# The skip term D*xi of a state-space block: added to y by VectorE instead of being scaled on ScalarE and transposed into the sum on TensorE

## The reference

```python
xi = silu(conv.transpose(0, 2, 1))
...
h = da * h + dbu                    # the scan over time, for 16 states
y = ys.transpose(1, 0, 2) + xi * Dp # the skip term
y = y * silu(z)
return jnp.einsum('bse,de->bsd', y, op_w)
```

## Time and profile before

| what | before |
|---|---|
| median of three runs (lowest, highest) | 8749.79 us (8738.89, 8761.13) |
| span of the profiled execution | 8758.3 us |
| VectorE busy | 6915.6 us, 79% |
| TensorE matmul busy, weight load busy | 7541.7 us (86%), 5200.9 us (59%) |
| GpSimd busy | 6082.7 us, 69% |
| ScalarE busy | 5521.0 us, 63% |
| mean granted TensorE clock | 0.943 of full |

### The profile page before, as it was taken

How to read it: one execution, slowest core, us unless ns; L and a number is a source line. 1 busy time by engine, 2 the same in 40 slices (tenths; PEclk the granted TensorE clock), 3 DMA queues, 4 the chain that set the end, 5 groups by cost and what they waited for, 6 DMA issues and landing times. The chain is left out here.

```text
span 8758.3 us, 163471 instructions
## 1 busy us (share of the span) xinstructions
PE 7541.7 (86%) x67488; PEld 5200.9 (59%) x67488; DVE 6915.6 (79%) x6906; ACT 5521.0 (63%) x8491; POOL 6082.7 (69%) x3204
## 2 busy tenths in 40 slices
PE   7886788888888888888888888888889888888879
PEld 4664466666664666666654666666654666666655
DVE  5887788888875588888875688888874688888873
ACT  5665676666654566666653666666654666667643
POOL 5883488888871588888861588888861588888861
PEclk8997899999999999999999999999999999999989
DMA  1111111111100111111100111111100111111100
GB/s 62 51 51 63 41 46 43 46 43 51 56 28 25 55 46 43 46 48 56 48 32 20 53 46 43 46 52 56 43 32 22 52 46 43 53 55 46 43 32 15
DMA packets 133156, 388.71 MB, mean 44 GB/s; under 512 B 49580, under 2 KB 78188, under 8 KB 95552
## 3 DMA queue, kind: packets, MB, share of 16 engines
q1 hardware_dynamic: 132416, 378.25, 12.0%
HBM read 364.97 MB, written 13.24 MB: 43 GB/s over the span
## 5 line engine op out<-in xcount | busy, mean ns | idle before, releaser
L1167 DVE TENSOR_TENSOR_SCAN arena<-arena,ps 128x512 f32<-128x512 f32 x4608 | 5493.0, 1254 | 1019.2 <-issue 822.1
L1418 POOL TENSOR_TENSOR arena<-arena 128x1024 f32<-128x1024 f32 x2240 | 5262.7, 2363 | 1115.4 <-DVE arena L1167 1087.0
L863 ACT ACTIVATE arena<-arena,rate 128x512 f32<-128x512 f32 (+1 forms) x4608 | 3040.6, 713 | 583.8 <-DVE arena L1167 579.3
L572 PEld LDWEIGHTS ps<-csts,arena 128*128 128x128 f32 x17920 | 2115.6, 146 | 514.3 <-issue 423.0
L572 PE MATMUL ps<-csts,arena 128*128 128x128 f32 x17920 | 2354.8, 283 | 4.8 <-POOL arena L1418 4.7
L555 PE MATMUL ps<-arena 32*128 32x128 f32 x36864 | 1434.8, 295 | 919.5 <-DVE arena L1167 910.1
L555 PEld LDWEIGHTS ps<-arena 32*128 32x128 f32 x36864 | 1213.0, 196 | 1176.6 <-DVE arena L1167 591.5
L1439 POOL TENSOR_TENSOR arena<-arena 128x512 f32<-128x512 f32 x288 | 372.2, 1292 | 797.9 <-ACT arena L997 564.9
L608 PE MATMUL ps<-arena 128*128 128x512 f32 x1152 | 661.3, 705 | 36.1 <-DVE arena L1177 21.3
L613 PE MATMUL ps<-arena 128*128 128x512 f32 x1120 | 554.4, 618 | 60.6 <-ACT arena L1005 49.2
L904 ACT ACTIVATE arena<-ps 128x512 f32<-128x512 f32 x280 | 167.1, 597 | 673.4 <-PE ps L572 672.9
(11 more groups left out here) (108 smaller groups left out, 6548.3 us busy)
## 6 DMA issues: line engine op xcount, KB each, us to landing
arena<-c_rows SPq DMA_DIRECT2D x288, 1024.0 KB, 4.6
arena<-ip_x SPq DMA_DIRECT2D x20, 512.0 KB, 3.9
arena<-ip_z SPq DMA_DIRECT2D x20, 512.0 KB, 4.0
arena<-op_w SPq DMA_DIRECT2D x20, 512.0 KB, 3.9
hT<-xT SPq DMA_DIRECT2D x16, 512.0 KB, 3.6
arena<-w SPq DMA_DIRECT2D x8, 1024.0 KB, 5.1
out<-arena SPq DMA_DIRECT2D x64, 128.0 KB, 1.7
arena<-xp_w SPq DMA_DIRECT2D x20, 160.0 KB, 2.5
```

The source lines that it names most:

```text
L572: i = nc.tensor.matmul(acc[:, b * P:(b + 1) * P], hs[:, place(n, v) + s, b * P:(b + 1) * P], eye, start=False, stop=(v + 1) % CU == 0 and ...
L863: nc.scalar.activation(o, i, ACT.Exp, scale=rate[:, ph.layer(n), g:g + 1]).then_inc(decay.sem, 1)
L1167: nc.vector.tensor_tensor_scan(hs[:, place(n, v) + g % 2, :], dA[:, g % RING, :], quad[:, g % Q::Q], init[:, n % 2, g:g + 1] if ph.main() ...
L1418: nc.gpsimd.tensor_tensor(hs[:, a:a + 2, :], hs[:, a:a + 2, :], Crep[:, 2 * pair:2 * pair + 2, :], ALU.mult).then_inc(prod.sem, 1)
```

## The change

ScalarE's scaling of `xs` (event `skip`, four a step) goes, and so do the four transposes at the start of each chunk's sum, 16 a step. In their place VectorE has a new event `skip` right in front of `gate`: one instruction that computes y = xs * D + y, from SBUF and PSUM to the same PSUM bank. `gate` waits for it. `xs` gets three buffers, and the last tap no longer waits for a sum. In the block's table `gate0` moves from unit 21 to unit 17, and `tap01` from unit 25 to unit 23. Attention's weights that lay over the first `xs` buffer now lie over the third, and SyncE waits for the last `skip` of the step before the last, instead of its last sum, before it loads them. The tables of the prefix get `skip` in front of each `gate` at the same unit.

```diff
-MAIN_ACT = {0: [("skip2", 0)], 2: [("z1", 1)], 3: [("skip3", 0)], 5: [("z2", 1)],
+MAIN_ACT = {2: [("z1", 1)], 5: [("z2", 1)],
...
-            13: [("sq", 2)], 15: [("soft", 1), ("rstd", 2)], 18: [("skip0", 1)], 23: [("xi0", 2)], 24: [("dxT0", 1)],
-            25: [("skip1", 1), ("xi1", 2)], 27: [("xi2", 2)], 28: [("dxT1", 1)], 30: [("xi3", 2)],
+            13: [("sq", 2)], 15: [("soft", 1), ("rstd", 2)], 23: [("xi0", 2)], 24: [("dxT0", 1)],
+            25: [("xi1", 2)], 27: [("xi2", 2)], 28: [("dxT1", 1)], 30: [("xi3", 2)],
...
@@ sum_pair, TensorE
                     pe.wait_ge(y_out.sem, y_out.at(ph, n, c))
-                    pe.wait_ge(skip.sem, skip.at(ph, n, c + 1))
-                    for b in range(NB):
-                        nc.tensor.matmul(acc[:, b * P:(b + 1) * P], xs[:, n % 2, c, b * P:(b + 1) * P], eye,
-                                         start=b == 0, stop=False, is_transpose=True)
...
@@ last tap, VectorE
-                        dve.wait_ge(summed.sem, summed.at(ph, m - 2, c * CU + 1))
-                        if ph.bk == 0 and m < 2:
+                        if ph.bk == 0 and m < XS:
...
@@ events, VectorE
+                elif name[:4] == "skip":
+                    y = job_bank(ph, f"yt{c}")
+                    await_done(dve, ph, m, f"yt{c}")
+                    nc.vector.scalar_tensor_tensor(y, xs[:, m % XS, c, :], Dall[:, ph.layer(m), c:c + 1], y,
+                                                   ALU.mult, ALU.add).then_inc(skip.sem, 1)
                 elif name[:4] == "gate":
                     dve.wait_ge(silu_z.sem, silu_z.at(ph, m, 1))
-                    await_done(dve, ph, m, f"yt{c}")
+                    dve.wait_ge(skip.sem, skip.at(ph, m, c + 1))
...
@@ SyncE
-                    sp.wait_ge(summed.sem, summed.at(ph, n - 1, UNITS))
+                    sp.wait_ge(skip.sem, skip.at(ph, n - 1, KI))
```

More of the change, by code:

```diff
@@ L30 @@
 ZS = 3
+XS = 3
 XP = 80
@@ L60 @@
 PRE_ACT_FIRST = {2: [("yev3", -1)], 9: [("yev0", 0)], 18: [("yev1", 0)], 25: [("yev2", 0)]}
-PRE_ACT = {5: [("sq", 1)], 6: [("dxT1", 0), ("skip1", 0)], 7: [("rstd", 1), ("skip2", 0)], 8: [("dxT2", 0)],
+PRE_ACT = {5: [("sq", 1)], 6: [("dxT1", 0)], 7: [("rstd", 1)], 8: [("dxT2", 0)],
            10: [("xi0", 1), ("xi1", 1)], 12: [("xi2", 1)], 13: [("dxT3", 0)], 15: [("xi3", 1), ("z0", 1)],
[2 rows of a table removed]
-PRE_DVE = {3: [("gate3", -1)], 5: [("res0", -1), ("res1", -1)], 9: [("norm0", 1), ("norm1", 1)],
[2 rows of a table added]
+PRE_DVE = {3: [("skip3", -1), ("gate3", -1)], 5: [("res0", -1), ("res1", -1)], 9: [("norm0", 1), ("norm1", 1)],
            11: [("tap00", 1), ("tap01", 1), ("tap02", 1)], 13: [("tap10", 1), ("tap11", 1), ("tap12", 1)],
            15: [("tap20", 1), ("tap21", 1), ("tap22", 1)], 17: [("tap30", 1), ("tap31", 1), ("tap32", 1)],
[1 row of a table removed]
[1 row of a table added]
 PRE_POOL = {4: [("dtx1", 0)], 7: [("dtx2", 0)], 10: [("dtx3", 0)], 23: [("dtx0", 1)]}
@@ L79 @@
 MAIN_ACT_FIRST = {2: [("yev3", -1)], 10: [("yev0", 0)], 18: [("yev1", 0)], 25: [("yev2", 0)]}
-MAIN_ACT = {0: [("skip2", 0)], 2: [("z1", 1)], 3: [("skip3", 0)], 5: [("z2", 1)],
+MAIN_ACT = {2: [("z1", 1)], 5: [("z2", 1)],
             6: [("silu_x", 1), ("z3", 1), ("silu_z", 0)], 8: [("dxT3", 0)], 9: [("xp", 1)], 10: [("bT", 1)],
[2 rows of a table removed]
[2 rows of a table added]
             31: [("dxT2", 1), ("z0", 2)]}
-MAIN_DVE = {1: [("tap22", 1), ("tap30", 1)], 3: [("tap31", 1), ("tap32", 1)], 7: [("gate2", -1)], 9: [("gate3", -1)],
[2 rows of a table removed]
+MAIN_DVE = {1: [("tap22", 1), ("tap30", 1)], 3: [("tap31", 1), ("tap32", 1)], 7: [("skip2", -1), ("gate2", -1)],
[3 rows of a table added]
             29: [("tap11", 2), ("tap12", 2)], 31: [("tap20", 2), ("tap21", 2)]}
@@ L256, in program @@
         xs_at = at[0]
-        xs = view(2, KI, T)
+        xs = view(XS, KI, T)
         zs_at = at[0]
@@ L301, in program @@
         fsq = save[:, 0, :][:, 0:KD * S // 2], save[:, 1, :][:, 0:KD * S // 2]
-        at[0] = xs_at
+        at[0] = xs_at + 2 * KI * T
         wq_s = view(KD, D)
@@ L573, in sum_pair @@
                                              hs[:, place(n, v) + s, b * P:(b + 1) * P], eye,
-                                             start=False, stop=(v + 1) % CU == 0 and s == 1 and b == NB - 1,
+                                             start=v % CU == 0 and s == 0 and b == 0,
+                                             stop=(v + 1) % CU == 0 and s == 1 and b == NB - 1,
                                              is_transpose=True)
@@ L618, in job @@
                     for k in parts:
-                        i = nc.tensor.matmul(o[0:XP, :], xpw[:, k, :], xs[:, par, k, :], start=k == 0, stop=k == KI - 1)
+                        i = nc.tensor.matmul(o[0:XP, :], xpw[:, k, :], xs[:, m % XS, k, :], start=k == 0, stop=k == KI - 1)
                 elif name == "bT":
@@ L1000, in event @@
                         nc.scalar.preload_act_table_set(LOG_EXP)
-                elif name[:2] == "dx":
+                else:
                     act.wait_ge(input_ready.sem, input_ready.at(ph, m - 1, (c + 1) * CQ))
@@ L1006, in event @@
                                          ).then_inc(read_of(ph, name), 1)
-                else:
-                    act.wait_ge(dtx_ready.sem, dtx_ready.at(ph, m, c + 1))
-                    nc.scalar.activation(xs[:, par, c, :], xs[:, par, c, :], ACT.Copy,
-                                         scale=Dall[:, ph.layer(m), c:c + 1]).then_inc(skip.sem, 1)
             def body(ph, n, part=range(UNITS)):
@@ L1171, in event @@
             def event(ph, m, name):
-                c, par = int(name[-1]) if name[-1].isdigit() else 0, m % 2
+                c = int(name[-1]) if name[-1].isdigit() else 0
                 if name[:4] == "norm":
@@ L1183, in event @@
                     acc_c, pad = job_bank(ph, f"xi{c}"), xpad[:, c % 2, :]
-                    o = xs[:, par, c, :] if k == 2 else acc_c
+                    o = xs[:, m % XS, c, :] if k == 2 else acc_c
                     if k == 0:
```

4 lines of the change are left out of this document (2 added, 2 removed), and 11 rows, old and new, of tables (MAIN_DVE, PRE_ACT, PRE_DVE).

## The result

The kernel after takes 8791.51 us (median of 4 runs, 8779.87 to 8801.11), the kernel before, on the same chip, 8744.34 us (4 runs, 8730.24 to 8761.13). The ratio is 1.0058, 95% interval 1.0040 to 1.0077. That is slower, by more than a measurement can miss; I had forecast 8744 us. The profiled execution of after spans 8792.3 us, 34.0 us more than that of before, at a mean granted clock of 0.936 instead of 0.943.

What follows compares the result with a forecast made beforehand. Quads of four scans, about 6.23 us at least because TensorE makes the next input only after the last scan, bound the kernel. Terms -15 + 7 + 6 - 4 = -6 us, from 8749.8, gave 8744 us; range 8670 to 8800.

Steps and rivals of the forecast that it cites:

- The quad as metronome, free gaps: VectorE's four-scan quads: TensorE's input holds each at about 6.23 us; skip fits the gaps, zero cost in 56 ordinary steps.
- Rival 3: VectorE is the bound, so all 207 us of added skip work come on top: 8957 us; chance 0.04.
- yt3's wait: Unit 9's quad: skip2 delays gate2, whose bank yt3 needs; costs 0.10 us a step, bounds 0.05 to 0.15.
- Unit 11's quad: TensorE, late there at full clock, loses four transposes; quad goes from 6.45 to 6.23 us, -0.22 us a step.
- tap10's wait: After gate1, tap10 waits 0.28 us for xi1's eviction; removing ScalarE's scaling saves 0.15 us a step, bounds zero to 0.28.
- The last step of a block: Fuller gaps after units 9 and 17: skip costs 0.74 and 0.9 us; 4 x 1.65 = +7 us.
- The drain: Behind a block's last scan, two skips are on the way to the residual: 4 x 2 x 0.74 = +6 us.
- The prefix: Six steps where TensorE is late after unit 27: removed transposes save 0.6 to 1.1 us each, less skip's cost: -4 us.
- After unit 3: TensorE's 1.01 us idle there only grows when four transposes go; removing them there was priced at nothing.
- rival 2: Longer TensorE idle after unit 3 lowers its clock: one further fall in three steps, +30 us, 8774 us; chance 0.12.

Runs made afterwards that it cites:

- `yt3` moved: Kernel after with TensorE's yt3 placed behind the two xp jobs of unit 8 instead of in front; 8740.64 us, ratio 0.9991 to before.
- after with fillers: Kernel after, yt3 left in place, plus 11 thrown-away constant matmuls a block step in six places where TensorE waits; 8686.59 us, ratio 0.9930 to before.
- the square: Four versions of after: transposes gone, yt3 waiting 8791.5 or moved behind xp 8740.6 us; transposes kept with result thrown away, waiting 8776.5 or moved 8754.4 us.
- before with fillers: Kernel before plus 11 thrown-away constant matmuls a block step in six places, nothing else changed; 8666.84 us, ratio 0.9907 to before.

## Why the prediction was wrong

By its own steps, in the order of the text.

- **The quad as metronome, free gaps.** Right. A quad with `skip` and `gate` in its gap is 6.23 us, and the same instruction in front of `gate3` cost nothing (ratio 0.9988). Of VectorE's 204 added us none had to be paid for its amount. Rival 3 (8957 us) is refuted. The Trainium skill ("Perfetto Trace Analysis", Identifying the Most-Contended Engine) takes the engine of highest occupancy, with TensorE judged by its weight loads, as the one to optimise first. Here that names VectorE, but its share went from 79% to 81% at no cost of its own, and the time followed TensorE's clock.
- **yt3's wait, 0.10 us, bounds 0.05 to 0.15.** Mis-sized: 0.24 us in each inner step without a fall, outside the bounds, 13 us instead of 6. The working had `skip` 0.74 and `gate` 0.66 back to back, 1.40 us. The trace shows 1.53 from `skip2`'s start to `gate2`'s end: a hand-over of 0.11 between two dependent VectorE instructions, and a `gate` of 0.69.
- **Unit 11's quad, -0.22 us.** -0.30, to 6.15; -17 us instead of -12. The 6.23 was not the least that a quad can take: before's own quads of unit 13 are 6.15 us in the mean.
- **tap10's wait, -0.15 us.** The number came out, the reason mostly not. Unit 27's quad is 0.16 shorter (6.40 to 6.24), and the taps' wait is down by 10.5 us in total. But the two kernels without ScalarE's scaling and with the transposes have this quad at 6.36, and before without the transposes has it at 6.32: by one execution each, the scaling alone is worth 0.04 and the transposes alone 0.08. With the falls away it is 6.16 us in before already, so that there is nothing to win. To call the term right by its size would be to take luck for it.
- **The last step of a block, +1.65 us.** The mechanism and size were right: the quads of units 9 and 17 together are 1.77 us longer in the mean of the four (7.34 and 7.47, from 6.57 and 6.47). The steps as wholes didn't grow (99.79 us without their last quad, from 99.94), because the later quads had fewer long ones in this execution. The drain, +6: right, 4 x 1.44 = 5.8 us from the last scan to the last `res`. The prefix, -4: -5.3 with what lies ahead of its first scan, but not where the sum had it. The six quads of unit 27 take 53.8 us together instead of 52.9. The gain is in the prefix's last step (134.1 us from 141.5), which is 135.7 us long too in the two kernels with one more VectorE instruction, whose prefix is that of before. That the total came near -4 is chance. The first steps of the blocks, priced at nothing, are 4 us shorter together; with `yt3` moved they are 5.5 us longer again, so that one execution settles nothing there.
- **After unit 3, "1.01 us of idle time, which only grows", priced at nothing.** This is the step that failed. It grows to 1.45 us, and 10 of 56 quads behind it ran at the lower clock for a while, 7.57 us instead of 6.23. That is the place and the mechanism of rival 2, which I had given 0.12, mainly for one row: after 1.81 us at 3873.84 the clock had stayed up. One row in which the clock did not fall is no evidence that such idle time is harmless, since the falls come in some of the steps only. The rule of the Trainium skill that I set aside ("TensorE: Matmul & The Clock Gate", the section on HAM oscillation) says that waiting between bursts sends TensorE's clock down; its own case has longer waits than these. The runs agree in the direction: with 0.44 us more of it in front of one input the clock fell there in some steps, and with the waits filled it stayed up.
- **Rival 2's arithmetic** priced a fall at 1.62 us and only in unit 5's stretch. In the quads of units 5, 9 and 17 one costs 1.3 to 1.7 us. In the mean over all places it is less, 0.8 to 0.9: the inner steps of after are 144.6 us longer than those of after with fillers, with 164 falls more, and those of before 111.6 us longer, with 134 more. But a fall in unit 5's quad came with others: in after a step with falls in 5, 9 and 17 is 5.2 us longer than one with none of them. The further falls, 35 in 56 steps, came in units 5, 9, 17 and 31. By the rival's own count, one in three steps, its 8774 us would have been nearer than my 8744.

So of the 47 us some 20 are the change itself, as far as the kernels with fillers show it (8686.6 against 8666.8), of which moving `yt3` takes back 14 (spans) to 23 us (medians). The other 27 or so (23 by the spans) are the clock's, by difference. That the time goes with the clock holds beyond the profiled executions. In 80 runs of before, beside the experiments, the mean granted clock is 0.940 to 0.948 and the time 8726 to 8766 us, with a correlation of -0.88; the four runs of after are at 0.935 to 0.939, below all of them.

**What stays open.** That wait and missing transposes together cost more than the two apart is shown by the times of the square. That the excess is falls of the clock rests on counts of one execution each. Why is not shown. Of the 13 in unit 9's quad 10 stand in a step with one in unit 5's, and the wait brings four there with the transposes or without (13 for 9, 5 for 1). Those of unit 17's quad (41 with both, 22, 29 and 24 in the other corners) stand next to neither edit, and the row before such a fall (an idle time of 1.26 us, in the earlier trace rows and in after's step alike) stands in steps with and without one. That a longer step shifts where the chip takes its decision is an idea that no run here tests.

## What to carry to other kernels

Where TensorE alternates between bursts of a few us and waits of 1 to 2 us, as here, its clock is part of the schedule. Before making its work lighter, count the low stretches by place, and compare kernels with the falls suppressed as well, since that shows what an edit costs by itself. An instruction added to an engine with slack is free by its amount, but look for the bank or buffer that its neighbour now frees later, and add the hand-over between dependent instructions to its length. When the waits can't be filled with real work, try a few matmuls whose result is thrown away, placed in the waits.

## What the hardware did that I had not expected

- **Useless matmuls make a kernel quicker.** 11 a step (0.60 us for the 128x256 one) took before from 8746.5 to 8666.8 us and after with `yt3` moved from 8740.6 to 8663.7; TensorE's granted clock in the inner steps went from 0.95 to 0.97 up to 0.99 to 1.00.
- **Much of the spread between runs is the clock's.** In 80 runs of before the time moves with the mean granted clock (correlation -0.88). With 7 falls in the inner steps the four runs of before with fillers lie within 6.3 us; four of before itself, with 141, lie within 30.9 us. It is not all of it: after with fillers (12 falls) still spreads over 12.3 us, and the version with fillers in the first 15 steps over 17.5.
- **Transposes hold the clock up as other matmuls do.** The four kept in front of the sum after unit 3 (0.60 us) took away all falls in the next quad, as the filler of 0.60 us did. The Trainium skill ("TensorE: Matmul & The Clock Gate", Part 4, PE-mode transpose) says that transposes don't count as a busy engine in the same way; the falls of unit 5's quad, 10 without and 0 with them, don't bear that out here.
